# The end of a four-layer attention and FFN kernel: ScalarE takes both pending down columns before its last rounding, VectorE's two low halves stand in a row, and the last half columns are dealt anew

## The reference

```python
x = x + xattn0(layernorm(x), ctx)                # softmax attention on ctx
x = x + ffn0(layernorm(x))                       # dense 512x512 plus routed LoRA
x = x + xattn1(layernorm(x), ctx, mask)          # 32 heads, 8 kv heads, q and k rms-normed
x = x + (silu(h @ gate) * (h @ up)) @ down       # h = layernorm(x); 4-bit weights in groups of 128, hidden 1792
```

## Time and profile before

| what | value |
|---|---|
| median of three runs | 871.88 us |
| the profiled execution's own time | 870.88 us |
| its span in the trace | 869.1 us |
| TensorE busy | 831.3 us, 96% |
| VectorE, ScalarE, GpSimd busy | 64%, 62%, 63% |
| first product that waits for D0's take | 850.79 us |
| first product that waits for E2's take | 855.04 us |
| first transpose | 859.48 us |

### The profile page before, as it was taken

The page is one execution under the profiler, slowest core; times in us unless marked ns, Lnnn a source line. Parts: engine busy times, 40 slices in busy tenths (PEclk is TensorE's granted clock), DMA queues, the critical chain, the costliest instruction groups (busy, mean ns, idle before and its releaser), DMA issues.

```text
span 869.1 us, 14112 instructions
## 1 busy us (share of the span) xinstructions
PE 831.3 (96%) x3984; PEld 678.0 (78%) x3984; DVE 556.4 (64%) x974; ACT 540.7 (62%) x1785; POOL 550.2 (63%) x557
## 2 busy tenths in 40 slices
PE   6899999999989999999999999999996899999995
PEld 5687888788778888888888888888884677777774
DVE  6505531433466666666666666666666799999996
ACT  4533672134677777777777667776775477667663
POOL 3332452113387777777777777776776368999985
PEclk9999999999999999999999999999999999999998
DMA  8411011003566666666667766667754123333302
GB/s 273 170 49 62 1 49 49 19 31 89 143 193 183 188 189 191 188 184 187 184 187 227 210 195 182 188 188 217 206 157 125 46 77 142 145 146 145 143 3 97
DMA packets 73223, 122.74 MB, mean 141 GB/s; under 512 B 8077, under 2 KB 45837, under 8 KB 73166
## 3 DMA queue, kind: packets, MB, share of 16 engines
q1 hardware_dynamic: 73166, 122.10, 46.5%
HBM read 86.41 MB, written 35.65 MB: 140 GB/s over the span
## 4 chain that ended last, share of the span: by engine, by line
PE 82%; DVE 7%; DMA 4%; POOL 2%; issue 2%; ACT 2%; SPq 1%; POOLq 0%; ACTq 0%; DVEq 0%
PE pair L1404 18%; PE pair L1405 18%; PE pair L1406 18%; PE pair L1560 9%; PE pair L1561 8%; PE pair L1650 6%; DMA land<-block_bounce 1%; DMA block_bounce<-tb 1%; PE pair L1421 1%; DVE kv L1268 1%; DVE st L1056 1%; DMA resid<-in_x_dram 1%; PE pair L1523 1%; PE pair L1460 1%; PE pair L1518 1%
## 5 line engine op out<-in xcount | busy, mean ns | idle before, releaser
L1404 PE MATMUL pair<-split,xnT_hi 128*128 128x512 f32 x288 | 114.2, 397 | 0.2 <-issue 0.2
L1405 PE MATMUL pair<-split,xnT_hi 128*128 128x512 f32 x288 | 112.1, 389 | 0.0
L1406 PE MATMUL pair<-split,xnT_lo 128*128 128x512 f32 x288 | 112.1, 389 | 0.0
L1404 PE MATMUL pair<-split,aoT_hi 128*128 128x512 f32 x256 | 100.1, 391 | 0.0
L1405 PE MATMUL pair<-split,aoT_hi 128*128 128x512 f32 x256 | 100.1, 391 | 0.0
L1406 PE MATMUL pair<-split,aoT_lo 128*128 128x512 f32 x256 | 100.0, 391 | 0.0
L895 ACT ACTIVATE prob<-pair,nmax 128x128 f32<-128x128 f32 x256 | 90.2, 363 | 15.3 <-DVE nmax L1232 14.8
L870 ACT ACTIVATE headT<-land 128x512 f32<-128x512 f32 x64 | 40.5, 632 | 94.7 <-DMA land<-block_bounce 72.0
L1560 PE MATMUL pair<-xnT_hi,split 128*128 128x512 f32 x224 | 91.2, 407 | 3.2 <-ACT kv L958 1.3
L649 POOL TENSOR_TENSOR prob<-prob,rinv 128x512 f32<-128x512 f32 x64 | 66.6, 1041 | 41.0 <-DVE rinv L1202 40.9
L1561 PE MATMUL pair<-xnT_lo,split 128*128 128x512 f32 x224 | 87.7, 391 | 0.0
(11 more groups left out here) (153 smaller groups left out, 2177.2 us busy)
## 6 DMA issues: line engine op xcount, KB each, us to landing
block_bounce<-tb SPq DMA_DIRECT2D x244, 128.0 KB, 2.3
land<-block_bounce SPq DMA_DIRECT2D x61, 512.0 KB, 3.4
raw<-in_wqo_dram SPq DMA_DIRECT2D x62, 256.0 KB, 3.0
kv<-in_ffn_w_dram SPq DMA_DIRECT2D x14, 768.0 KB, 4.4
kv<-in_ffn_z_dram SPq DMA_DIRECT2D x14, 768.0 KB, 5.6
resid<-in_x_dram SPq DMA_DIRECT2D x2, 1024.0 KB, 9.0
kv<-in_ctx_dram SPq DMA_DIRECT2D x1, 2048.0 KB, 10.8
out_dram<-resid SPq DMA_DIRECT2D x8, 256.0 KB, 2.3
```

What stands on the lines that cost most here:

```text
L1404: pe.matmul(dst, l_hi, r_hi, start=first, stop=False)
L1405: pe.matmul(dst, l_hi, r_lo, start=False, stop=False)
L1406: return pe.matmul(dst, l_lo, r_hi, start=False, stop=last)
```

## The change

Three things move in the end of the kernel.

1. ScalarE takes D0 and now D1 too (into the free temporary `tmp_c`) right after silu, ahead of the first rounding. GpSimd adds the D1 temporary onto column 1 of `accT` (a new 128x1024 add, new semaphore `s_p1`), between the add of unit 12's column 0 and that of E3.
2. VectorE no longer takes D1; its two low halves follow one another, then E2's take.
3. The half column (second half, column 0) goes from ScalarE and GpSimd to VectorE, which has six of them now, and waits once more on `s_pa` and `s_p1`; ScalarE and GpSimd keep two.

TensorE's order stays; its waits are rewritten to the new counts.

```diff
             pool.wait_ge(s_ta, by_scalar(LAST, 9) + 1)
+            pool.tensor_tensor(accT[:, 1, :], accT[:, 1, :], tmp_c, ALU.add).then_inc(s_p1, 1)
+            pool.wait_ge(s_ta, by_scalar(LAST, 9) + 2)
             pool.tensor_tensor(accT[:, 3, :], accT[:, 3, :], tmp_b, ALU.add).then_inc(s_pb, 1)
-            for e, (h, c) in enumerate(((0, 0), (0, 3), (1, 0))):
+            for e, (h, c) in enumerate(((0, 0), (0, 3))):
                 last_added(e, h, c)
...
+            take(LAST, None, 9, tmp_a, down_s[:, 1 - LAST % 2, 0:1])
+            take(LAST, None, SUM, tmp_c, down_s[:, 1 - LAST % 2, 1:2])
             last_hi(0)
-            take(LAST, None, 9, tmp_a, down_s[:, 1 - LAST % 2, 0:1])
             last_hi(1)
...
-            for e, (h, c) in enumerate(((0, 0), (0, 3), (1, 0))):
+            for e, (h, c) in enumerate(((0, 0), (0, 3))):
                 act.wait_ge(s_it, item(LAST, 13) + KT * h + LAST_DOWN.index(c) + 1)
                 if e == 0:
                     act.wait_ge(s_pa, LAST - 1)
+                else:
+                    act.wait_ge(s_p1, 1)
...
             last_lo(0)
-            take_down(LAST, None, SUM, 1, False)
             last_lo(1)
...
-            for h, c in ((0, 1), (0, 2), (1, 3), (1, 1), (1, 2)):
+            for h, c in ((0, 1), (0, 2), (1, 0), (1, 3), (1, 1), (1, 2)):
...
+                if c == 0:
+                    dve.wait_ge(s_pa, LAST - 1)
+                if c == 1:
+                    dve.wait_ge(s_p1, 1)
...
                         elif c == 3:
-                            pe.wait_ge(s_tv, by_vector(LAST, SIDE))
+                            pe.wait_ge(s_ta, by_scalar(LAST, 9) + 1)
                         elif c == 1:
-                            pe.wait_ge(s_tv, by_vector(LAST, SIDE) + 1)
+                            pe.wait_ge(s_tv, by_vector(LAST, 8) + 1)
                         else:
-                            pe.wait_ge(s_ta, by_scalar(LAST, 9) + 1)
+                            pe.wait_ge(s_ta, by_scalar(LAST, 9) + 2)
...
-                    pe.wait_ge(s_tv, by_vector(LAST, SIDE) + 1 + (2, 5)[h])
-                    pe.wait_ge(s_pa, LAST + h)
+                    pe.wait_ge(s_tv, by_vector(LAST, 8) + 1 + (2, 6)[h])
+                    pe.wait_ge(s_pa, LAST)
```

More of the change, by code:

```diff
@@ L333, in cross_attention_ffn @@
         s_pb = sem("down_added_from_b")
+        s_p1 = sem("last_down_one_added")
         s_oc = sem("out_copied")
@@ L712, in last_added @@
                 tmp, done = (tmp_a, s_pa) if c == 0 else (tmp_c, s_pb)
-                pool.wait_ge(s_ta, by_scalar(LAST, 9) + 2 + e)
+                pool.wait_ge(s_ta, by_scalar(LAST, 9) + 3 + e)
                 pool.wait_ge(done, LAST - 1)
@@ L1384, in _ @@
             dve.wait_ge(s_ds, UNITS)
-            for h, c in ((0, 1), (0, 2), (1, 3), (1, 1), (1, 2)):
+            for h, c in ((0, 1), (0, 2), (1, 0), (1, 3), (1, 1), (1, 2)):
                 dve.wait_ge(s_it, item(LAST, 13) + KT * h + LAST_DOWN.index(c) + 1)
-                dve.wait_ge(s_tv, by_vector(LAST, SIDE) + 1)
+                dve.wait_ge(s_tv, by_vector(LAST, 8) + 1)
+                if c == 0:
+                    dve.wait_ge(s_pa, LAST - 1)
+                if c == 1:
+                    dve.wait_ge(s_p1, 1)
                 if c == 3:
```

## The result

The changed kernel is slower. The comparison of eight runs of each gives a ratio of 1.0038 (95% interval 1.0021 to 1.0056), so 1.8 to 4.9 us, 3.3 in the middle. The medians are 875.66 us (872.28 to 878.08) and 871.69 us (869.37 to 873.91). Against the forecast of +2.0 us (873.9) the direction is right and the size small. The interval of the ratio takes in +2.0 near its lower end. The measured median of 875.66 lies above the stated range, which ends at 875.2; the ratio applied to the forecast's starting point of 871.88 gives 875.2, its edge.

The account below looks back on a forecast made before the run. TensorE, busy 96% of the span, was taken as the bound nearly everywhere, but VectorE's chain near the end. +1.80 us for the third half column and +0.2 for the clock gave +2.0: 873.9 from 871.88, range 871.5 to 875.2.

Parts of the forecast that it names:

- The first low half is held by D1's add, the second by E3's: VectorE's low halves each wait for a running GpSimd add, ending 0.56 us after it; chance 0.78.
- Who comes next: After the first low half, GpSimd's E3 add, ready at 852.3, goes ahead of VectorE's second low half, at about 852.8.
- They take turns: VectorE subtractions with both inputs in SBUF and GpSimd adds alternate, so both low halves pay for an add each.
- +1.80 us for the third half column: TensorE's third half column of unit 13 starts at 856.84 instead of 855.04, held to +-0.15 us.
- +0.2 us for the twelve matmuls: Unit 13's last twelve matmuls take 4.65 instead of 4.44 us as the clock falls earlier; bounds -1.6 and +0.7.
- 0 for what follows the first transpose: The 9.6 us of transposes, output adds and stores at the end stay as they are.
- a few tenths more: Extra time if TensorE's clock stays at half into the transposes.
- The half columns' move costs 0, up to 0.5 at full clock: VectorE's six half columns finish before the second half's transposes; cost 0.5 us only if all twelve matmuls ran at full clock.
- The rival with one hold: Only one low half waits for an add; third half column 0.3 us earlier than before, time 871.8; chance 0.13.
- The clock forgives it: Both low halves are held but the twelve matmuls run at full clock: +0.2 us, 872.1; lower end of the likeliest case.
- the rival without a hold: D1's add doesn't hold VectorE's low halves; third half column 1.93 us earlier, time 869.5; chance 0.09.
- the clock may then stay full: Without holds, full clock for part of the twelve matmuls gains another 0.5 us.

Follow-up runs that it names:

- the first three experiments: Three edits of the changed kernel: GpSimd's D1 add left out; E3's add after the second low half; hidden halves in PSUM, the last 0.9985 of the kernel before.

## Why the prediction was right, and where its size was off

- *The first low half is held by D1's add, the second by E3's*: right. Forecast 2.5 and 2.8 us, measured 2.57 and 2.85. The prediction read it from the earlier trace rows, and the first three experiments show it: no add beside the low halves, no hold; one add moved out of the way, one hold fewer; one input in PSUM, no hold beside a running add.
- *Who comes next*: right. "They take turns" rested on one row with another form of instruction; the run with E3's add moved back confirms that the second hold is E3's. Whether the engines take turns or the first to arrive goes first is open: in every row here the one that got in had also been ready first.
- *+1.80 us for the third half column*: measured +1.87.
- *+0.2 us for the twelve matmuls*: this term was mis-sized, by 0.77 us. "I expect the fall to come in the gaps, before the twelve, and take 4.65": the fall did come in the first gap, but the clock then stayed at half through all twelve, in three profiles of three, and they took 5.29 us, more even than the upper bound of 5.1. That bound (12 x 0.43 is 5.16) left out the first matmul behind the gap, spaced 0.59 us instead of 0.43. The 4.65 has no sum behind it and takes the clock to come back inside the twelve. The four matmuls between the gaps ran at half clock too, so that the second gap, put at 2.9 us, was 1.89. It may be this second gap that kept the clock down: in the run with E3's add moved back, which has only the first, the clock came back among the twelve, once. Against the mean of three profiles of before the term is +0.97.
- *0 for what follows the first transpose*: measured +0.22, no more than the kernel before varies there (9.62 to 9.89). The prediction named "a few tenths more" if the clock stayed at half into the transposes, and didn't add them; in the changed kernel the first 0.4 us of transposes are at half clock.
- *The half columns' move costs 0, up to 0.5 at full clock*: right; with TensorE kept busy 0.15 us of wait shows at full clock, with the move alone none.
- The rival with one hold has its picture in the run with E3's add moved back: third half column H+7.29, 0.24 us before the old H+7.53, where 0.3 was forecast. It did not come about in the changed kernel.
- "The clock forgives it" was put at +0.2; with the clock kept full by spare matmuls the measured end was +0.7 (22.30 - 21.58). It didn't come about by itself.
- Of the rival without a hold, "the clock may then stay full" is answered both ways. With the changed kernel's order and no hold the third half column came 2.0 us earlier than before (forecast 1.93). Once the holds were gone the clock still fell in the three runs with a gap of 1.10 us and another of 0.76 to 1.06 us left before the twelve; it stayed full in the two where E2's take between the halves had closed the gap before the twelve.

What decides whether the clock falls stays open. The spare matmuls show what it costs, not the condition: the same gaps gave different clocks in the kernel before and in the run with the half column moved.

## What to carry to other kernels

Before moving work to GpSimd, list the VectorE instructions with both inputs in SBUF that will run beside it: each waits for the end of a running GpSimd add (here 0.55 us beyond it, 2.57 and 2.85 us instead of 0.68), and GpSimd's next add goes ahead of VectorE's next such instruction if it is ready first. Taking one of the two inputs from PSUM removed the wait here without changing the order. At a kernel's end, price TensorE's gaps twice, once for themselves and once for the matmuls behind them at half clock.

## What the runs showed of the hardware that I had not expected

- The length of the gaps alone does not tell the clock. With gaps of 1.10, 0.46 and 1.06 us (D0's take first, one profile) the twelve matmuls took 5.29 us, and a gain of 1.0 us in the order vanished. With gaps of 1.75 to 1.79 and 2.06 to 2.09 us they took 4.18 to 4.44 in three profiles of the kernel before, and in the run with the half column moved they ran at full clock.
- The first matmul at half clock behind a gap is followed by the second only after 0.59 us, against 0.43 in the stream; at full clock that spacing is 0.34 us, against 0.23.
- Nineteen spare matmuls, 2.33 and 2.44 us of needless work inside the two gaps, made the changed kernel's end 2.25 us shorter.
